# Inverting a mixture-of-experts token table in two passes instead of one, with shared feed-forward steps and the last weight preparation at other places

## The reference, cut to what matters

```python
x = L0_attn_x                                   # (8, 512, 256) float32, 4096 tokens
x = x + layernorm(linear_attention(layernorm(x)))   # 32 heads of 8, no softmax
h = layernorm(x)
shared = (silu(h @ Gs.T) * (h @ Us.T)) @ Ds.T        # hidden size 704, every token
probs = softmax(h @ gate_w.T); topw, topi = top_k(probs, 2); topw /= topw.sum() + 1e-20
routed = sum_e ffn_e(h) * comb[:, e]                  # 8 experts, two per token
return x + layernorm(shared + routed)
```

## Time and profile before

| | |
|---|---|
| median of 3 runs | 855.06 us (852.76 to 855.31) |
| the profiled execution | 854.16 us, of which the span from first to last instruction is 852.4 us |
| mean granted TensorE clock | 0.978 of full speed |
| busy: PE, PEld, DVE, ACT, POOL | 784.7, 643.7, 583.6, 487.4, 290.2 us |

### The profile page before, as it was taken

One profiled execution on the slowest core, in us unless ns is written; L12 is line 12 of the kernel. 1 busy time (PEld: TensorE's weight loads), 2 busy tenths in 40 slices (PEclk: granted clock), 3 DMA queues, 4 the chain that ended last, 5 costly groups with the idle time before them and its releaser, 6 DMA issues.

```text
span 852.4 us, 21050 instructions
## 1 busy us (share of the span) xinstructions
PE 784.7 (92%) x6573; PEld 643.7 (76%) x6582; DVE 583.6 (68%) x1588; ACT 487.4 (57%) x1073; POOL 290.2 (34%) x316
## 2 busy tenths in 40 slices
PE   6989999999999998666999999999999999999991
PEld 2547777777777776444788888888888888888880
DVE  5758989898989888894787444555555555555553
ACT  4355848575766675421566555565656565656562
POOL 3011010101010000072265555555555555555542
PEclk9999999999999999997999999999999999999996
DMA  4114444343526161502244555646464646474733
GB/s 192 50 50 156 119 153 126 141 145 118 162 93 191 64 188 43 149 9 68 48 66 77 100 76 72 125 74 146 75 148 74 145 72 143 71 147 71 145 44 95
DMA packets 102692, 90.10 MB, mean 106 GB/s; under 512 B 63761, under 2 KB 94225, under 8 KB 101457
## 3 DMA queue, kind: packets, MB, share of 16 engines
q1 hardware_dynamic: 87648, 68.45, 27.5%
q0 software_dynamic: 14976, 20.78, 17.1%
HBM read 48.70 MB, written 27.39 MB: 89 GB/s over the span
## 4 chain that ended last, share of the span: by engine, by line
PE 72%; DVE 16%; ACT 5%; issue 4%; POOL 2%; DMA 1%; SPq 0%; ACTq 0%; DVEq 0%; POOLq 0%
PE ps L918 41%; PE ps L933 19%; PE ps L1002 4%; PE ps L1034 3%; DVE wgu L1289 3%; PE ps L996 2%; DVE hf L1229 2%; ACT wgu L778 2%; DVE wdn L1289 1%; DVE st L1405 1%; DVE wdn L1538 1%; PE ps L963 1%; DVE st L1209 1%; DVE hT L1239 1%; PE ps L1005 1%
## 5 line engine op out<-in xcount | busy, mean ns | idle before, releaser
L918 PE MATMUL ps<-xhl,wgu 128*128 128x256 f16 x3102 | 387.6, 275 | 12.3 <-DMA xhl<-attw 6.7
L918 PEld LDWEIGHTS ps<-xhl,wgu 128*128 (+1 forms) x3102 | 304.5, 99 | 56.0 <-issue 8.6
L1229 DVE SCALAR_TENSOR_TENSOR hf<-ps,sc,silu 128x256 f32<-128x256 f32 x330 | 159.6, 484 | 188.8 <-ACT silu L730 163.4
L730 ACT ACTIVATE silu<-ps,sc 128x256 f32<-128x256 f32 x275 | 130.4, 474 | 236.2 <-PE ps L918 236.1
L933 PE MATMUL ps<-wdn,hT 128*128 (+1 forms) x1870 | 252.8, 273 | 9.6 <-DVE hT L1239 7.2
L933 PEld LDWEIGHTS ps<-wdn,hT 128*128 128x128 f16 x1870 | 181.9, 98 | 35.1 <-DVE hT L1239 6.3
L673 POOL DMA_INDIRECT acc_d<-ysb,gst x78 | 128.8, 1651 | 44.5 <-POOL gst L669 30.9
L606 POOL TENSOR_TENSOR rstd<-ve,mhalf 128x4 f32<-128x4 f32 (+1 forms) x32 | 30.7, 960 | 294.6 <-DVE ve L1214 272.9
L1239 DVE TENSOR_TENSOR hT<-hf,hT 128x256 f16<-128x256 f32 x275 | 114.7, 417 | 1.7
L744 ACT CAST hT<-hf 128x256 f16<-128x256 f32 x275 | 109.7, 399 | 8.8 <-DVE hf L1229 7.1
L662 POOL DMA_INDIRECT attw<-xn_d,gst x78 | 80.1, 1027 | 44.5 <-POOL gst L658 32.6
(11 more groups left out here) (245 smaller groups left out, 768.0 us busy)
## 6 DMA issues: line engine op xcount, KB each, us to landing
wgu<-in_gu SPq DMA_DIRECT2D x8, 1408.0 KB, 6.4
att<-in_x SPq DMA_DIRECT2D x16, 512.0 KB, 5.5
wdn<-in_dn SPq DMA_DIRECT2D x8, 768.0 KB, 8.1
x_d<-att SPq DMA_DIRECT2D x8, 512.0 KB, 2.9
xn_d<-wgu SPq DMA_DIRECT2D x8, 512.0 KB, 3.3
acc_d<-ysb SPq DMA_DIRECT2D x16, 256.0 KB, 3.3
att<-x_d SPq DMA_DIRECT2D x8, 512.0 KB, 4.9
att<-acc_d SPq DMA_DIRECT2D x7, 512.0 KB
```

The source lines that it names most:

```text
L730: a.activation(silu[:, c % 2 * TW:(c % 2 + 1) * TW], gu_ps[c % 2][:, 0:TW], ACT.Silu, scale=scale_of(slot, 0)).then_inc(silu_made, 1)
L918: ins = te.matmul(o, slot_gu(slot, hw, k, j), x(hx, k), start=(n == 0), stop=(n == len(TERMS) - 1))
L1229: v.scalar_tensor_tensor(out=hf[lo:P, c % 2 * TW:(c % 2 + 1) * TW], in0=up, scalar=scale_of(slot, 1, lo, P), in1=silu[lo:P, c % 2 * TW:(c ...
```

## The change

The list of tokens is inverted in two passes. The first covers the 16 columns of the first eight tiles, whose slots are put at fixed places (expert e's slots begin at e * 4096, `expert_at`), so that it needs neither the counts nor the order. It lies in TAIL, in front of shared steps H 8 to H 11. The second covers the other 62 columns and lies in routed tiles 0 to 3 (HOT_AT, INVERT_AT). The token number is now multiplied into the columns' one-hots (`one_hi`), and the rows' one-hots (`one_lo`) are made whole on DVE, one instruction a group; GpSimd makes none. The ranks come from matmuls with repeated operands that add up in PSUM (`ranks`), where the scan was. `route_segments` and `route_order` come after the last shared step, and their matmul after the first chunk of tile 0; `route_table` in chunk 2. Weights and positions of part 0 follow D 11 of the last attention batch, which has H 11 two steps earlier. Slots 7 and 8 are prepared in chunks 1 to 26 and 25 to 39 (PREP_AT). The raw weights of slot 8 are loaded ahead of the transposes of tile 5, after the second pass. The first two gathers take their indices straight from `idx`. PE issues six matmuls of 512 columns (`keep_busy`) ahead of tile 0, and waits for `eid_made` only at tile 8. The attention part of batches 1 to 7 is the same; at the start POOL makes one more constant and two casts.

The diff, cut to its core (function bodies that are removed stand in the kernel above):

```diff
+PART_B = ((0, B - 1), (B - 1, B))
+PART = tuple((NT * lo, NT * hi) for lo, hi in PART_B)
...
-TAIL = [("route_top1", 1), ("route_top2", 1), ("G", 0), ("H", 0), ("route_slots",), ("G", 1), ("G", 2), ("H", 1), ("D", 0), ("G", 3),
-         ("D", 1), ("route_order",), ("G", 4), ("G", 5), ("H", 2), ("G", 6), ("G", 7), ("route_positions",), ("H", 3), ("route_table",),
-         ("H", 4), ("G", 8), ("D", 2), ("one_hots", 0), ("G", 9), ("H", 5), ("H", 6), ("invert", 0), ("one_hots", 1), ("H", 7),
-         ("invert", 1), ("D", 3), ("D", 4), ("one_hots", 2), ("invert", 2), ("one_hots", 3), ("H", 8), ("invert", 3), ("one_hots", 4),
-         ("invert", 4), ("one_hots", 5), ("D", 5), ("invert", 5), ("G", 10), ("one_hots", 6), ("D", 6), ("H", 9), ("D", 7), ("invert", 6),
-         ("one_hots", 7), ("invert", 7), ("G", 11), ("route_indices",), ("H", 10), ("D", 8), ("H", 11), ("D", 9), ("D", 10), ("D", 11)]
...
+         ("turn2",), ("G", 10), ("xhl",), ("H", 10), ("rows2",), ("G", 11), ("D", 8), ("logits",), ("H", 11), ("route_slots", 0), ("D", 9), ("logits_out",),
+         ("D", 10), ("route_probs", 1), ("D", 11), ("route_weights", 0), ("route_positions", 0)]
...
+TAIL = [("G", 0), ("H", 0), ("one_lo", 0), ("route_norm", 1), ("G", 1), ("route_top1", 1), ("G", 2), ("H", 1), ("D", 0), ("route_top2", 1), ("G", 3),
+        ("H", 2), ("D", 1), ("route_slots", 1), ("one_lo", 1), ("route_weights", 1), ("G", 4), ("H", 3), ("D", 2), ("route_positions", 1), ("one_hi", 0),
+        ("G", 5), ("H", 4), ("D", 3), ("one_lo", 2), ("one_lo", 3), ("invert", 0), ("invert", 1), ("G", 6), ("H", 5), ("D", 4), ("one_lo", 4), ("one_lo", 5),
+        ("G", 7), ("H", 6), ("D", 5), ("invert", 2), ("invert", 3), ("one_lo", 6), ("one_lo", 7), ("one_hi", 1), ("G", 8), ("H", 7),
+        ("invert", 4), ("invert", 5), ("invert", 6), ("invert", 7), ("route_indices", 0), ("D", 6), ("G", 9), ("H", 8), ("D", 7), ("route_counts",), ("G", 10),
+        ("H", 9), ("D", 8), ("G", 11), ("H", 10), ("D", 9), ("H", 11), ("D", 10), ("D", 11), ("route_segments",), ("route_order",)]
...
+PREP_AT = ((1, 4, 6, 8, 10, 19, 21, 23, 24, 26), (25, 27, 29, 30, 32, 33, 35, 37, 38, 39))
+PREP_STEPS = (("max", 0), ("max", 1), ("max", 2), ("diag", 0), ("spread", 0), ("scale", 0), ("prep", 0), ("prep", 1), ("prep", 2), ("prep", 3))
+LATE = {divmod(at, FC): (step[0], s, step[1]) for s in range(NPRE, NSLOT) for at, step in zip(PREP_AT[s - NPRE], PREP_STEPS)}
...
+HOT_AT = (3, 5, 7, 9, 11, 13, 15, 17)
+LATE |= {divmod(at, FC): ("one_hi", 0, g) for g, at in enumerate(HOT_AT)}
+LATE |= {(0, 2): ("table", 0, 0)}
+LATE |= {divmod(HOT_AT[-1] + 3, FC): ("indices", 0, 0)}
+INVERT_AT = {divmod(at + 2, FC): g for g, at in enumerate(HOT_AT)}
...
+        STATIC = E * TT
+        REST = NCOL - STATIC
...
+        oh_first = attw[:, 1056:1568].bitcast(F16).rearrange("p (m j c) -> p m j c", m=2, j=NTB)
+        oh_rest = [attw[:, 1568 + 248 * r:1816 + 248 * r].bitcast(F16).rearrange("p (m j c) -> p m j c", m=2, j=OHB) for r in range(2)]
...
-            sp.wait_ge(logits_made, B)
-            sp.dma_start(last_gu, gu_in[E]).then_inc(last_loaded, 16)
-            sp.dma_start(last_dn, dn_in[E]).then_inc(last_loaded, 16)
...
+            def store_comb(n):
...
+                sp.wait_ge(comb_made, n + 1)
+                lo, hi = PART[n]
+                sp.dma_start(xn2_d[lo * P:hi * P, D:D + E].rearrange("(t p) e -> p t e", p=P),
+                             part_of(r_t, n).rearrange("p (t e) -> p t e", e=E)).then_inc(comb_stored, 16)
+            store_comb(0)
+            store_comb(LAST)
...
             for i in range(NTILE):
+                if i == 5:
+                    sp.wait_ge(rest_used, OHG)
+                    sp.dma_start(last_gu, gu_in[E]).then_inc(last_loaded, 16)
+                    sp.dma_start(last_dn, dn_in[E]).then_inc(last_loaded, 16)
...
-            for step in TAIL:
-                if step[0] == "one_hots":
...
-                    pool.wait_ge(remainders_made, 1)
...
-                    for h in range(OHB - POOL_H, OHB):
-                        j = OHB * step[1] + h
...
-                            ins = g.tensor_scalar(oh_lo[step[1] % OHR][:, m, h, :], iota16[:, :], lof[:, n:n + 1], tokf[:, j:j + 1], ALU.is_equal, ALU.mult)
...
-                g.tensor_copy(idxc[:, 2 * r:2 * r + 2], idx[:, bass.ds(i * TT, TT)]).then_inc(idxc_made, 1)
-                pool.wait_ge(idxc_made, i + 1)
...
+                rows = idx[:, i * TT:(i + 1) * TT] if first else idxc[:, 2 * r:2 * r + 2]
+                if not first:
+                    g.tensor_copy(rows, idx[:, bass.ds(i * TT, TT)]).then_inc(idxc_made, 1)
+                    pool.wait_ge(idxc_made, i - 1)
+                    passed(pool)
                 for t in range(TT):
                     g.indirect_dma_start(xg[:, r, t, :], None, xn2_d[:, :],
-                                         bass.IndirectOffsetOnAxis(ap=idxc[:, 2 * r + t:2 * r + t + 1], axis=0)).then_inc(xg_loaded[r], 16)
+                                         bass.IndirectOffsetOnAxis(ap=rows[:, t:t + 1], axis=0)).then_inc(xg_loaded[r], 16)
...
+                if i + 3 == E:
+                    pool.wait_ge(idx_made, 4)
...
+            def ranks(n):
...
+                pe.wait_ge(m_made, n + 1)
...
+                te.matmul(dst, upper16, m16[:, E * t0:E * t1], start=True, stop=False)
+                for b in range(PART_B[n][0]):
+                    te.matmul(dst.rearrange("p (t e) -> p t e", e=E), ones16[:, :], each(bsum16[:, E * b:E * b + E], t1 - t0), start=False, stop=False)
+                for t in range(t0, t1 - 1):
+                    ins = te.matmul(dst[:, E * (t + 1 - t0):].rearrange("p (t e) -> p t e", e=E), ones16[:, :], each(m16[:, E * t:E * t + E], t1 - 1 - t),
+                                    start=False, stop=(t == t1 - 2))
+                ins.then_inc(ranked, 1)
...
+            def invert(n, g):
...
+                pe.wait_ge(onehot_lo_made, g + 1)
+                if n == 0:
+                    pe.wait_ge(first_hi_made, 1 if OHB * g < PART[0][1] else 2)
+                else:
+                    pe.wait_ge(rest_hi_made, g + 1)
+                for h in range(OHB):
+                    for m in range(2):
+                        hi = oh_first[:, m, OHB * g + h, :] if n == 0 else oh_rest[g % 2][:, m, h, :]
+                        ins = te.matmul(inverted(n), oh_lo[g][:, m, h, :], hi, start=(g == 0 and h == 0 and m == 0), stop=(g == OHG - 1 and h == OHB - 1 and m == 1))
+                ins.then_inc(rest_used if n else first_used, 1)
...
-                    pe.wait_ge(m_made, 2)
-                    x2_ready(pe, B - 1)
-                    te.matmul(att_ps[0][:, 0:256], upper[:, :], r_m, start=True, stop=True)
-                    te.matmul(att_ps[0][:, 256:512], ones[:, :], r_m, start=True, stop=True).then_inc(counted, 1)
...
+                    ranks(step[1])
+                if kind == "route_counts":
+                    pe.wait_ge(logits_made, B)
+                    for b in range(B):
+                        ins = te.matmul(att_ps[3][:, E * b:B * E].rearrange("p (t e) -> p t e", e=E), ones16[:, :], each(bsum16[:, E * b:E * b + E], B - b),
+                                        start=(b == 0), stop=(b == B - 1))
+                    ins.then_inc(counted, 1)
                 if kind == "invert":
...
-            pe.wait_ge(eid_made, 1)
+                    invert(0, step[1])
+            pe.wait_ge(h_made, FC * 2 * B + 1)
+            keep_busy(6)
...
+                    if isinstance(i, int) and (i, c) == (0, 0):
+                        pe.wait_ge(order_made, 1)
+                        te.matmul(att_ps[2][:, 0:NCOL], ones[:, :], picked, start=True, stop=True).then_inc(order_spread, 1)
+                    if isinstance(i, int) and (i, c) in INVERT_AT:
+                        invert(1, INVERT_AT[i, c])
...
+                    rl(v.tensor_tensor(mm, o1, o2, ALU.add))
...
+                        v.tensor_reduce(sums.rearrange("p (b e) -> p b e", e=E), mm.rearrange("p (b t e) -> p b e t", t=NT, e=E), AX.X, ALU.add).then_inc(m_made, 1)
+                if kind == "route_weights":
...
+                    dve.wait_ge(ranked, n + 1)
+                    at = expert_at.rearrange("p (o e) -> p o e", o=1).to_broadcast([P, count, E])
+                    v.tensor_tensor(te8(xx), te8(rank_bank(n)), at, ALU.add).then_inc(rank_read, 1)
+                    dve.wait_ge(rank_read, n + 1)
+                    v.tensor_tensor(cc, o1, xx, ALU.mult)
+                    rl(v.tensor_tensor(pr, o2, xx, ALU.mult))
+                    v.tensor_reduce(posf[:, t0:t1], te8(cc), AX.X, ALU.add)
+                    rl(v.tensor_reduce(posf[:, NTB + t0:NTB + t1], te8(pr), AX.X, ALU.add))
...
+            def one_hi(dst, lo, hi, c0, c1, made):
...
+                h4 = hif16.rearrange("p (m j o) -> p m j o", m=2, o=1)[:, :, lo:hi, :].to_broadcast(shape)
```

(65 more changed lines are left out.)

203 lines of the change are left out of this document (86 added, 117 removed), and 4 rows, old and new, of the table LAST_ORDER.

## The result

The changed kernel takes 842.49 us (median of 4 runs, 840.84 to 844.47), the kernel before 854.70 in the same session (4 runs, 852.76 to 855.31): ratio 0.986, 95% interval 0.984 to 0.988, so 10 to 13 us faster. Forecast were 843.5 us and a range of 838.0 to 850.5.

A forecast was written before the change was run, and what follows sets the result against it. PE, busy 92%, was taken to bound the kernel, but DVE the stretch up to the lists. Gains of 14.6 less 2.4 and 1.1 made 11.1 us: 854.16 to 843.1, some 843.5 as median, range 838 to 850.5.

The forecast's parts named there:

- DVE's queue: Up to the finished lists: 32.4 us leave, 19.9 enter, so lists are ready 12.5 us earlier, at X = 377.2.
- The hand-over: From lists to PE: first routed matmul at X + 9.6 = 386.8, 12.8 us earlier, 0.9 from the dropped index copy.
- The clock: First 48 routed matmuls: 2.0 of the 3.15 us lost to PE's slow start come back, as its last gap shrinks.
- The wait for the order: After the first routed chunk PE waits for segments and order, now behind DVE's last H: 0.2 us, at worst 2.2.
- The second pass on PE: Routed tiles: 64 added matmuls cost PE 2.2 us and the order's matmul 0.2.
- DVE in tiles 0 to 6: 12.8 us more DVE work makes PE stall 4.5 us against 3.4 now: cost 1.1, bounds 0 to 8.
- The last load, POOL: Routed tiles: slot 8's later weight load and POOL copies slowed beside `one_hi` were both taken to cost nothing.
- From tile 7 on: Sign: from routed tile 7 both kernels must be alike; a difference there would break the whole account.
- 1: Rival: PE and its round trips hold TAIL, which shrinks by 6.5 instead of 12.5 us: 849.5; chance 0.13.
- 2: Rival: the routed tiles become DVE's; of 12.8 added us some 7 show instead of 1.1: 849.5; chance 0.12.
- 3: Rival: slot 8's load at a quarter of its pace makes DVE stand 17 us in the routed tiles: 860; chance 0.06.
- 4: Rival: something else holds the first gather, so earlier lists leave PE's gap and slow start: 850; chance 0.04.

The follow-up runs named there:

- second trace: The changed kernel run again with no edit, because its one trace seemed of a rare kind: 842.39 us, ratio 0.986 to the kernel before.
- first trace: The changed kernel's first profiled execution, the fastest of its four runs; their median is 842.49 us.
- a4_pe_twice: The changed kernel with each matmul of invert's second pass issued twice, the copy into columns nobody reads: 845.21 us, 2.8 slower than the changed kernel.

## Why the prediction was right, point by point

The mechanism came as forecast, and the size too, but the size partly by luck: several terms were off in ways that cancel.

- **DVE's queue.** Predicted 32.4 us out, 19.9 in, lists at 377.2. Measured 377.8 in the second trace, 375.8 in the first. Moving H 8 to H 11 back ahead of the lists gave 8.7 us away, which shows the one-to-one rule. I had priced only H 8 and H 9 as moved (1.4 us), since H 10 and H 11 stood behind the lists already.
- **The hand-over.** First routed matmul predicted at 386.8, measured 386.5 and 385.9; 13.1 and 13.7 us earlier against 12.8. The copy's 0.9 us fits its own experiment (1.4 less between lists and PE, 0.9 in the medians).
- **The clock.** Predicted 2.0 us of a loss of 3.15. Two readings were mixed there: 8.31 us runs from the first start to the last end, and 0.1075 us a matmul is a count over a stretch that cuts into matmuls at both ends. From start to start the loss is 8.15 - 5.24 = 2.9 us, and in both traces of the changed kernel all but 0.1 of it is gone. This term was too low by 0.9.
- **The wait for the order.** This was the weak term: 0.2, measured 1.3 in the typical trace (1.4 from start to start). The step that failed is "DVE is done at about X + 6.6 + 4.5 = X + 11.1 against X + 10.9": `upper` was written at 389.2, which is X + 11.4, while PE asked for it at X + 10.2, since it starts at X + 8.7 and not at X + 9.6. The prediction's "at worst 2.2, if PE starts at X + 8.9" leaves out the 1.3 us of the first chunk; by its own numbers a start at X + 8.9 gives 0.9. When PE starts late (first trace, X + 10.1) the wait is nothing: start and wait trade against each other, and so neither is worth much alone.
- **The second pass on PE.** Predicted 2.4; eight groups at 0.23 us are 1.8, and the order's matmul is 0.3: 2.1. a4_pe_twice bears it out with 1.7.
- **DVE in tiles 0 to 6.** Predicted stalls of 4.5 against 3.4, a cost of 1.1. The view of the waits gives 1.9 + 0.7 against 2.2 + 1.2, which would be a gain, but it counts idle time from a matmul's modelled end, so that each stall shows some 0.16 us short and the smallest not at all. Counted from start to start (what exceeds 0.109 us between two matmuls), the stalls behind the first 48 matmuls are 5.0 us in the changed kernel, in twelve places, against 4.2 before, in five; 3.7 of the 5.0 stand ahead of gate and up matmuls, where PE waits for `hf`, near the 4 to 5 that were named. So DVE's cost is 0.8. The wait for the diagonal is gone, as forecast. That the margin is nearly used up was understated: the next 5.6 us cost 3.0 to 5.0. (The prediction's 1.3 us for chunk 5 of a tile is too long beside its own 1.82 on average, which leaves 1.1; the average is what its sum of 75 us uses.)
- **The last load, POOL.** Nothing, as taken; the load has 5.7 us in hand. A POOL copy does get slower beside `one_hi`: one lasts 1.10 us where 0.18 is the line's median.
```profile
406.43 1.10 POOL L692 COPY gst<-attw 128x2 int32<-128x2 int32 x1 [2.11 <-ACT ysb L785]
```
DVE's two-input `one_hi` runs from 406.82 to 408.20, over most of that copy. It is hidden. The Trainium skill (SBUF — State Buffer, Who interferes with whom) has a DVE instruction with two SBUF inputs contend with a GpSimd instruction that reads SBUF. The trace agrees, now for the added instructions themselves.
- **The sum** for the second trace: 13.1 (start) + 2.9 (clock) - 1.4 (wait for the order) - 2.1 (second pass, order's matmul) - 0.8 (DVE) = 11.7. Its last four terms make 1.4 us, which is just what PE's first to last grew by (433.87 to 435.25), so nothing is left over there. The span fell by 852.4 - 841.5 = 10.9; the other 0.8 lies behind PE's last group (19.7 us against 18.9), which the change does not touch and where all fourteen traces scatter from 18.7 to 19.7. The prediction had 12.8 + 2.0 - 0.2 - 2.4 - 1.1 = 11.1: the order's 1.2 us too little and the 0.9 too little for the clock nearly cancel. That two errors cancel is luck. So is half a microsecond of the forecast: 843.1 and the median's 0.9 make 844.0, and the 843.5 written down is not that sum.
- **From tile 7 on** the two had to be alike, and PE's matmuls are, to 0.01 us.

Rivals: 1 is refuted by the waits in TAIL (PE waits 8.8 us for DVE, DVE 0.2 for PE); 2 is not what happened, but its mechanism governs the next microsecond; 3 did not occur, and where it was made to happen it cost more than DVE's stand (5.4 us of stand, 7.6 on PE's path); 4 refuted, the gather starts 0.3 us behind the lists.

## What to carry to other kernels

When a serial chain on one engine gates a big consumer, sort that engine's queue by who needs what: work that the gate does not need is worth moving behind it even if it is then late itself; here four H's with the waits between them were 8.7 us when they stood ahead of the gate. Before adding work to an engine that feeds the bound one, double a piece of it and look at the bound engine's own path from its first to its last instruction, in which less scatters than in the whole time: a busy share of 88% was already at the edge, and a wait that vanishes at one place for such an engine comes back at the next. Read more than one execution before you trust a wait of 1 us: the same instructions put the lists at 375.8 or at 377.8.
